# Softmax sums of a wide cross-attention: accumulators as the stationary operand, reciprocals on 128x4, spread by transfers

## What is computed

```python
q = _split_heads(jnp.einsum('bnd,df->bnf', x, Wq))           # 8 sequences, 256 queries, 16 heads of 64
kv = jnp.einsum('bmc,cf->bmf', context, Wkv)                 # 1601 keys of the context
...
k = jnp.concatenate((nk, k), axis=-2)                        # one null key: 1602
q = q * scale
sim = jnp.einsum('bhid,bhjd->bhij', q, k)
attn = jax.nn.softmax(sim, axis=-1)
out = jnp.einsum('bhij,bhjd->bhid', attn, v)
out = jnp.einsum('bnf,fd->bnd', out.transpose(0, 2, 1, 3).reshape(b, -1, INNER), Wout)
```

## Time and profile before

| | us |
|---|---|
| median of three runs | 4947.77 |
| lowest and highest | 4946.61, 4952.59 |
| the profiled execution | 4972.34 |
| its span, first to last instruction | 4970.5 |
| outside the span | 1.8 |
| stage 4, first queries to last output copy | 858 to 2581 |

### The profile page before, as it was taken

How to read it: one execution, slowest core, us unless ns; L and a number is a source line. 1 busy time by engine, 2 the same in 40 slices (tenths; PEclk the granted TensorE clock), 3 DMA queues, 4 the chain that set the end, 5 groups by cost and what they waited for, 6 DMA issues and landing times. The chain is left out here.

```text
span 4970.5 us, 77611 instructions
## 1 busy us (share of the span) xinstructions
PE 4080.7 (82%) x29258; PEld 2235.3 (45%) x29323; DVE 3509.2 (71%) x5453; ACT 2512.4 (51%) x3544; POOL 1406.8 (28%) x1033
## 2 busy tenths in 40 slices
PE   5659796999999999999968986848995768888883
PEld 3645334666666666666643333423443332222231
DVE  5569444999997777777774455757764658888868
ACT  2133242666666666666641233535662436766772
POOL 0000300677776666666657011000000100000000
PEclk5579897999999999999978997978995779999996
DMA  0024001111110000000013016326540433223300
GB/s 19 1 109 165 27 0 57 41 47 47 34 41 1 14 1 14 14 1 1 1 55 138 0 34 138 48 46 87 78 60 4 105 71 59 46 41 54 49 2 9
DMA packets 144611, 218.53 MB, mean 44 GB/s; under 512 B 20442, under 2 KB 109036, under 8 KB 143556
## 3 DMA queue, kind: packets, MB, share of 16 engines
q1 hardware_dynamic: 136548, 197.22, 17.4%
q0 software_dynamic: 6528, 16.42, 1.4%
q10 hardware_dynamic: 1184, 0.12, 0.0%
HBM read 154.00 MB, written 56.69 MB: 42 GB/s over the span
## 5 line engine op out<-in xcount | busy, mean ns | idle before, releaser
L3114 POOL TENSOR_TENSOR arena<-arena 128x512 f32<-128x512 f32 (+1 forms) x768 | 1159.2, 1511 | 562.5 <-ACT arena L3070 503.2
L2544 ACT ACTIVATE arena<-ps 128x1024 f32<-128x1024 f32 (+1 forms) x688 | 703.9, 1024 | 335.3 <-PE ps L2469 324.8
L2562 DVE TENSOR_REDUCE arena<-ps 128x2 f32<-128x826 f32 (+1 forms) x576 | 565.0, 981 | 189.1 <-PE ps L2415 181.3
L3130 DVE TENSOR_TENSOR arena<-arena 128x1024 f32<-128x1024 f32 (+1 forms) x448 | 678.3, 1553 | 9.8 <-ACT arena L3097 9.8
L3152 DVE TENSOR_TENSOR arena<-ps,arena 128x512 f32<-128x512 f32 (+1 forms) x768 | 529.6, 690 | 121.1 <-ACT arena L3064 86.9
L2415 PE MATMUL ps<-arena 48*128 48x413 bf16 (+3 forms) x1920 | 435.1, 333 | 131.2 <-DVE arena L2562 65.4
L3064 ACT ACTIVATE arena<-ps 128x1024 f32<-128x1024 f32 (+1 forms) x448 | 412.6, 961 | 210.1 <-PE ps L2991 204.8
L2972 PE MATMUL ps<-arena 128*128 128x256 f32 (+1 forms) x1664 | 443.2, 394 | 45.5 <-DVE arena L3138 40.2
L3070 ACT ACTIVATE arena<-arena 128x1024 f32<-128x1024 f32 (+1 forms) x448 | 430.1, 993 | 93.1 <-DVE arena L3130 89.7
L2991 PE MATMUL ps<-arena 64*128 64x256 f32 (+1 forms) x3328 | 430.8, 392 | 23.4 <-DVE arena L3152 11.2
L2488 PE MATMUL ps<-arena 128*9 128x256 f32 (+2 forms) x5504 | 435.4, 389 | 10.1 <-ACT arena L2532 7.2
(11 more groups left out here) (650 smaller groups left out, 5895.6 us busy)
## 6 DMA issues: line engine op xcount, KB each, us to landing
wide_keys<-arena SPq DMA_DIRECT2D x27, 800.5 KB, 3.4
arena<-wide_keys SPq DMA_DIRECT2D x27, 800.5 KB, 4.3
arena<-in_ctx_feat SPq DMA_DIRECT2D x12, 1601.0 KB, 10.6
arena<-ctx_parts SPq DMA_DIRECT2D x96, 200.1 KB
arena<-ctx_parts SPq DMA_DIRECT2D x192, 100.1 KB
arena<-in_ctx SPq DMA_DIRECT2D x16, 768.0 KB
arena<-diff_att_stack SPq DMA_DIRECT2D x60, 192.0 KB
ctx_parts<-arena SPq DMA_DIRECT2D x24, 400.2 KB, 3.5
```

Source lines behind the costliest of these rows:

```text
L2544: act.activation(self.prob[0:rows, u % 3, :], self.ps[0:rows, 2 * (u % 2):2 * (u % 2) + 2, :].rearrange("p n c -> p (n c)"), ACT.Exp).then ...
L2562: ins = dve.tensor_reduce(dst[:, :, j // 2], self.ps[:, 4:6, 0:hi - lo], AX.X, ALU.max)
L3114: pool.tensor_tensor(acc[0:rows, u % 2, :], before, sc[0:rows, u % 2, t, :], ALU.add).then_inc(added, 1)
L3130: dve.tensor_tensor(e, e, mb[0:rows, u % 2, None, :].to_broadcast([rows, n, 2 * S]), ALU.subtract).then_inc(sub_done, 1)
```

## The change

The maximum starts with tile 1 and takes tile 0 from ACT's copy in `sc`, so the copy L3149 goes and `max_done` counts twelve per unit. The sums over partitions are made with `acc` as the stationary operand, four blocks of 128 x 128, and one column of ones as the moving one: the 512 sums of a unit come out as 128 partitions x 4 columns. DVE takes the reciprocal of that (128 x 4). SP stores the 512 reciprocals as rows to a DRAM tensor, element by element, waits for that, and loads each head's row of 256 back onto 64 partitions (two transfers). DVE multiplies four slots after the sums, at the start of pair P10 or P2, ahead of the subtractions; `inv` is doubled. In the ring the chunks of keys come first, then the values, and the queries last; `bcast` stands behind two keys where there are chunks and behind one elsewhere. The key `out` comes one pair later. SP's loop runs over all units: the transfers of unit u - 4, then the early keys of unit u, then a context after every eighth.

```diff
-            last = x - self.LAG - 5 - 6
+            last = x - self.LAG - 5 - 8
...
-        return turn + keys[0:2] + bcast + keys[2:] + late
+        keys = chunks[0:1] + values[0:1] + chunks[1:] + values[1:] + query
+        between = 2 if chunks else 1
+        return turn + keys[0:between] + bcast + keys[between:] + late
...
+            def spread_inverse(u):
+                sp.wait_ge(inv_ready, u + 1)
+                if u >= 2:
+                    sp.wait_ge(inv_spread, 32 * (u - 1))
+                    sp.wait_ge(normed, u - 1)
+                sp.dma_start(inv_rows[u % 2].rearrange("j p -> p j"), inv_q[:, u % 2, :],
+                             allow_slow_non_contiguous=True).then_inc(inv_stored, 16)
+                sp.wait_ge(inv_stored, 16 * (u + 1))
+                for e in range(2):
+                    row = inv_rows[u % 2, 2 * e:2 * e + 2, :].rearrange("j p -> (j p)")[None, :]
+                    sp.dma_start(inv[e * HW:(e + 1) * HW, u % 2, :], row.to_broadcast([HW, S])).then_inc(inv_spread, 16)
+            for u in range(2, plan.UNITS + 4):
+                if u >= 4:
+                    spread_inverse(u - 4)
+                if u < EARLY_UNITS:
+                    early_keys(u)
                 if u % HP == 1 and u // HP + 1 < B:
                     fetch(u // HP + 1)
...
-                    for e in range(2):
-                        ins = pe.matmul(ps[e * HW:(e + 1) * HW, 6 + u % 2, S:2 * S], ones[:, :],
-                                        acc[:, u % 2, e * S:(e + 1) * S], start=True, stop=True)
+                    for j in range(4):
+                        ins = pe.matmul(ps[:, 6 + u % 2, S + j:S + j + 1], acc[:, u % 2, j * P:(j + 1) * P],
+                                        ones[:, 0:1], start=True, stop=True)
...
+                for u in plan.ended(s, plan.LAG + 6):
+                    dve.wait_ge(inv_spread, 32 * (u + 1))
+                    if u >= HP:
+                        dve.wait_ge(ring_ready, plan.index["out", u // HP - 1] + 1)
+                    dve.tensor_tensor(oT[:, u % HP, :], ps[:, 6 + u % 2, 0:S], inv[:, u % 2, :], ALU.mult
+                                      ).then_inc(normed, 1)
...
+                        if t == 0:
+                            continue
...
-                        if t == 0:
+                        if t == 1:
                             if u >= 2:
                                 dve.wait_ge(ring_ready, plan.index["turn", u - 2] + 1)
-                            ins = dve.tensor_copy(most, got)
+                            before = sc[0:rows, u % 2, 0, :].rearrange("p (e q) -> p e q", e=2)
                         else:
-                            dve.wait_ge(max_done, len(tiles) * u + t)
-                            ins = dve.tensor_tensor(most, got, most, ALU.max)
-                        ins.then_inc(max_done, 1)
+                            dve.wait_ge(max_done, last_tile * u + t - 1)
+                            before = most
+                        dve.tensor_tensor(most, got, before, ALU.max).then_inc(max_done, 1)
...
                     dve.wait_ge(sums_done, u + 1)
-                    link(dve.reciprocal(inv[:, :], ps[:, 6 + u % 2, S:2 * S]))
-                    if u >= HP:
-                        dve.wait_ge(ring_ready, plan.index["out", u // HP - 1] + 1)
-                    dve.tensor_tensor(oT[:, u % HP, :], ps[:, 6 + u % 2, 0:S], inv[:, :], ALU.mult).then_inc(normed, 1)
+                    if u >= 2:
+                        dve.wait_ge(inv_stored, 16 * (u - 1))
+                    dve.reciprocal(inv_q[:, u % 2, :], ps[:, 6 + u % 2, S:S + 4]).then_inc(inv_ready, 1)
```

More of the change, by code:

```diff
@@ L2848, in ring_of @@
     def ring_of(self, s):
-        turn, keys, bcast, late = [], [], [], []
+        turn, query, chunks, values, bcast, late = [], [], [], [], [], []
         for x in (s, s + 1):
@@ L2853, in ring_of @@
             if u + 1 < self.UNITS and k == 0:
-                keys.append(("q", u + 1))
+                query.append(("q", u + 1))
             if 0 <= x < self.SLOTS and x % 14 < len(self.tiles):
-                keys.append(("v", x // 14, x % 14))
+                values.append(("v", x // 14, x % 14))
             if EARLY_UNITS <= u + 1 < self.UNITS and k in self.CHUNK_AT:
-                keys.append(("k", u + 1, self.CHUNK_AT[k]))
+                chunks.append(("k", u + 1, self.CHUNK_AT[k]))
             if k == 1 and 0 <= u - 1 < self.UNITS:
@@ L2894, in stage4 @@
         acc = st.sb("acc", [P, 2, 2 * S])
-        inv = st.sb("inv", [P, S])
+        inv_q = st.sb("inv_q", [P, 2, 4])
+        inv = st.sb("inv", [P, 2, S])
+        inv_rows = env.nc.dram_tensor("wide_inv_rows", (2, 4, P), F32, kind="Internal").ap()
         oT = st.sb("oT", [P, HP, S])
@@ L2904, in stage4 @@
         pv_done, sums_done, normed = st.sem("pv_done"), st.sem("sums_done"), st.sem("normed")
+        inv_ready, inv_stored, inv_spread = st.sem("inv_ready"), st.sem("inv_stored"), st.sem("inv_spread")
         block = st.block()
@@ L2933, in _ @@
             fetch(1)
-            for u in range(2, EARLY_UNITS):
-                early_keys(u)
+            def spread_inverse(u):
[14 more added lines that the diff above has]
+                    early_keys(u)
                 if u % HP == 1 and u // HP + 1 < B:
                     fetch(u // HP + 1)
-            for b in range((EARLY_UNITS - 2) // HP + 2, B):
-                fetch(b)
         @block.tensor
@@ L2986, in scores @@
                     before, step = plan.unit(s, 2)
-                    pe.wait_ge(max_done, len(tiles) * before + plan.tiles_of(step)[-1] + 1)
+                    pe.wait_ge(max_done, last_tile * before + plan.tiles_of(step)[-1])
                 for t in plan.tiles_of(k):
@@ L3022, in _ @@
                     elif key[0] == "turn":
-                        pe.wait_ge(max_done, len(tiles) * (key[1] + 1))
+                        pe.wait_ge(max_done, last_tile * (key[1] + 1))
                         bank = ring_bank(key)
```

## The result

| | us |
|---|---|
| before, median of four runs | 4948.75 (4946.61 to 4952.59) |
| after, median of four runs | 5134.18 (5125.82 to 5141.89) |
| ratio | 1.0373, 95% interval 1.0353 to 1.0394 |
| the profiled execution of after, and its span | 5141.89, 5140.1 |

The changed kernel is 185 us slower. The forecast was 4914 and the range ended at 4952, so both missed; what came is rival (c), the late round trip, and it cost far more than the 4992 it was priced at.

What follows compares the result with a forecast made beforehand. PE was taken to bound late units, while early DVE and PE wait for each other in turn. Early 26 us plus late 14 minus 6 at the stage's end gave 34 us gained: 4914 us, range 4868 to 4952.

Steps and rivals of the forecast that it cites:

- rival (c): Round trip late at 10.5 us: DVE stands 3 us per early unit, about nothing late; 4992 us, chance 0.13.
- the price of the store: Storing 512 reciprocals to DRAM: 4.6 us, interpolated by piece count, within a 7.1 us round trip (ends 3.6 and 13).
- The loads: Two loads bringing reciprocals back, 64 rows each: 1.8 us each, the second issued about 0.4 behind the first.
- The return of DVE: DVE reaches the product 7.1 to 7.8 us after the reciprocal early, about 10 late; the trip just fits, nothing charged.
- the order: Ring with chunks first, queries last: removes three waits of PE late, 0.86 us a unit, 32 us in all.
- the sums: Eight one-column records on PE instead of four: 0.5 us more a unit, covered early, 18 us lost late.
- The stage's end: Behind the last unit nothing hides the round trip: 6 us lost, between 3 and 13.
- The loss in P10: Early pair P10 gets the product ahead of its subtractions, and the maxima end last there: a loss of 0.4 us.
- PE waiting on ACT in P6 longer than now: Listed as a sign of being wrong; early pair P6 was forecast unchanged, with a wait moving to the queries.
- the 2.25 us of DVE's removed work: Early, per unit: reciprocal 1.58 plus copy of tile 0 0.67; 2.0 us per two units counted, 26 us in all.
- (a): DVE was the only early bound: all 2.25 us a unit come back, early units of 22 us; 4882 us, chance 0.14.
- (b): POOL's additions and DVE's subtractions take turns: early units gain 0.3 us at most, 24 us each; 4932 us, chance 0.15.

Runs made afterwards that it cites:

- e8: The changed kernel storing only the first two of four rows of reciprocals, 256 pieces of 4 bytes: 5176.74 us, ratio 1.044.
- e9: The changed kernel with its 512 store pieces of 4 bytes set 64 bytes apart, loads reading other data: 4891.71 us, ratio 0.987.
- e10: The changed kernel with its 512 store pieces of 4 bytes set 512 bytes apart, loads reading other data: 4910.93 us, ratio 0.990.
- e2: The changed kernel with the reciprocals stored as 128 pieces of 16 bytes instead of 512 of 4: 4894.21 us, ratio 0.987.
- e5: The kernel before with the ring's new order alone, the copy of tile 0 kept: 4905.53 us, ratio 0.991.

## Why the prediction was wrong, step by step

**The step that failed is the price of the store.** It was interpolated by the number of pieces between 128 in 1.8 us and 1024 in 8.3, both of them loads, and came to 4.6; the store took 8.1. Its upper end, 8.3, was right, but the count was the wrong axis: e8 against the changed kernel and e9 against both show that. The Trainium skill's rule that was cited there, one descriptor per element for a non-contiguous last dimension (DMA: Bandwidth & Descriptors, Rules for kernel authors), warned in the right place; its count of descriptors does not give the time, since 512 of them took 1.8 us in e9. The loads had been put too low as well: 3.8 us to landing at the median (2.5 to 5.9) against 1.8, and still 2.6 to 3.0 behind the shorter stores. The row of 1.8 is a load of 128 pieces at the program's start; these read one row and spread it over 64 partitions, two in series. That the row is freshly written is not the reason: the loads of e9 and e10 read other data and took 2.6. So of the 6.0 us by which the trip outgrew 7.1, the store brought 3.5 and the loads about 2.

**The return of DVE was right early and wrong late.** Early it is 7.0 or 7.75 us after the reciprocal, where 7.1 to 7.8 stood. The margin was therefore known to be nil, and a trip whose two ends were 3.6 and 13 should not have been charged nothing in the sum. Late "about 10" had been given; it is again 7.0 or 7.75, in all but the last of the 33 units.

**Rival (c) had the mechanism early, not late, and was too cheap.** At a trip of 13.1 its early stall would be 5.3 to 6. The waits between 950 and 1580 (as in the listing of the late part) show 6.1 a unit, and the units are 5.6 longer than e2's:

```profile
DVE arena L3146 <- DMA arena<-wide_inv_rows: 127.9, 21, 7.2
```

"About nothing late" rested on the return of about 10 us, so on idle time of DVE between the reciprocal and the product. It is not there; idle time only covers a wait that stands where the idle time is. This wait stood ahead of the subtractions, and ACT's in-order queue carried it to PE: 2.6 us a late unit more than in e2, 37 x 2.6 = 96 us. With 26 x 5.6 = 145 early and 7 at the stage's end that is 248, where the medians of the changed kernel and e2 lie 240 apart.

**What hung on the clock was not in the sum at all.** PE's pauses of 4 us were followed by stretches at 1.2 GHz, visible as 0.90 over the early part, above. The same stretch of e2:

```profile
950.00:1580.00 630.00, 613.15 (x4196) 426.38 (x4195) 549.89 (x585) 436.99 (x616) 500.99 (x319) 1.00 0.14 42
```

Per unit PE is busy for 528.91 / 630 x 28.55 = 24.0 us in the changed kernel and for 613.15 / 630 x 22.97 = 22.4 in e2, with the same work (153 records of matmuls a unit in both). By this reckoning 1.6 of the 5.6 us are matmuls at the lower clock.

**The rest of the sum had the right signs and was too low.** From e2: early 1.24 x 26 = 32 us gained against 26; late 0.81 x 37 = 30 against 14, since the order brought 0.98 (0.86 forecast) and the sums cost 0.17 (0.5 forecast). Their eight records take 0.95 us in the trace against 1.15, and the four before took 0.65:

```profile
2229.26 0.95 PE L3065 MATMUL ps<-arena 128*128 128x1 f32 x8
```

So 0.3 of it shows in the records, and part of that is hidden. The stage's end lost 11.5 us in the changed kernel (sums to projection 14.98 us against 3.44), inside the 3 to 13 given, and 4.6 in e2.

**By pairs**, e2 against before, medians in us from PE's first scores of a pair to those of the next: P0 9.65 to 7.78 (forecast -1.5, measured -1.9); P8 7.75 to 7.26 (-0.6, -0.5); P10 6.05 to 5.56 (+0.4, -0.5); P6 6.65 to 7.60 (unchanged, +0.95). The loss in P10 did not come, and the loss that came was in P6, which the prediction had named as a doubt ("PE waiting on ACT in P6 longer than now") and left out of the sum. The two errors nearly cancel. And the 2.25 us of DVE's removed work were one figure, though its parts differ: the copy's 0.67 brought nothing beside the long reciprocal, and the reciprocal's 1.58, with the new sums and the later product, 1.0. The other 0.3 of the early gain came from the order, which was in no term.

Of the other rivals, (a) would need early units of 22 us and (b) of 24: with the round trip out of the way they are at 22.97, the forecast's 23.3 or a little better. (b)'s price is out, its mechanism is not. The 24.0 us took an undisturbed subtraction at 1.35; those that no addition touches take 1.21 in the kernel before, as do the two of 2.35 us in the late listing above, which POOL leaves alone, beside 3.43 for the two under its additions. With 1.21 the sum is 12 x 1.27 + 6 x 1.21 + 0.68 = 23.2, and the short units are at 22.97. In e2 between 950 and 1550 subtractions and additions overlap in 82 stretches; undisturbed, their instructions would add up to 424 us, and the stretches last 392, so the two engines come close to taking turns. As PE is busy for 613 of 630 us in e2 (row above), no run tells which of the two holds the early unit at 22.97.

## What to carry to other kernels

Before an engine waits for a transfer's round trip, find where the wait stands in each in-order queue that follows, and ask for slack on the worst price and not on an interpolated one: here 7 to 7.8 us of slack met 13.1 us of trip, and one pair more of distance was worth 230 us. Price a store by how many of its pieces are neighbours in DRAM, not by how many there are; in these stores of 1 to 2 KB, 16 bytes a partition, or elements set apart, cost about a fifth of the same elements side by side. A part that pays in one stretch and costs in another can be switched between them, and an engine's idle time is no cover for a wait that stands ahead of work another engine needs.

## What the runs showed that was not expected

The time of a store went from 8.1 to 1.8 us by moving its 4-byte pieces from side by side to 64 bytes apart, and to 8.15 by leaving out half of them: less data was no faster.

The ring's order also took away a drop of the clock that the kernel before had once in eight units. Three times between 900 and 1480 PE paused for 1.88 us and the granted clock then read 0.50; pauses of up to 1.96 elsewhere in that stretch brought no drop. In e5 the longest pause there is 1.54, and the clock reads 1.00 throughout. Stretches of 2 us of the kernel before, then of e5 at the same times (not at the same place of the program, since its units are shorter):

```profile
1190.00:1192.00 2.00, 0.31 (x1) 0.30 (x2) 2.00 (x3) 0.93 (x1) 1.91 (x1) 1.00 0.00 0
1192.00:1194.00 2.00, 2.00 (x8) 1.70 (x7) 1.83 (x4) 0.78 (x3) 1.78 (x3) 0.51 0.00 0
```

```profile
1190.00:1192.00 2.00, 2.00 (x10) 1.50 (x12) 1.91 (x3) 1.12 (x3) 2.00 (x2) 1.00 0.00 0
1192.00:1194.00 2.00, 2.00 (x20) 1.46 (x20) 2.00 (x2) 1.31 (x3) 0.41 (x1) 1.00 0.00 0
```

PE is busy for 0.31 of 2 us ahead of the drop in the first; in the second there is neither pause nor drop.
